# Routed experts computed on per-expert slot tiles instead of for every token

## The reference, cut to what matters

```
def _L2_ffn_ref(x, w_gate, wi_0, wi_1, wo):          # 8 experts, top 2, hidden 256
    logits = xf @ w_gate
    top_logits, top_idx = top_k(logits, 2)
    weights = softmax(top_logits)
    out = sum over the two experts e of a token:
          weights * ((silu(x @ wi_0[e]) * (x @ wi_1[e])) @ wo[e])

def _L3_ffn_ref(x, gate_w, shared_gate_w, shared_gate_up_w, shared_down_w, w13, w2):
    shared = (silu_and_mul(x @ shared_gate_up_w.T) @ shared_down_w.T) * sigmoid(x @ shared_gate_w.T)
    probs = softmax(x @ gate_w.T); routing_weights, selected = top_k(probs, 2)   # 8 experts, hidden 352
    out = shared + sum over e of w_e * (silu_and_mul(x @ w13[e].T) @ w2[e].T)
```

## Time and profile before

| | |
|---|---|
| median of 3 runs | 3531.37 us (3529.96 to 3534.61) |
| the profiled execution, its own time | 3534.85 us |
| its span (first to last instruction) | 3533.0 us |
| TensorE matmul busy | 3068.1 us, 87% |
| VectorE / ACT / GpSimd busy | 51% / 36% / 27% |
| mean granted TensorE clock | 0.932 |
| DMA | 185.23 MB, mean 52 GB/s |

### The profile page before, as it was taken

How to read it: one execution, slowest core, us unless ns; L and a number is a source line. 1 busy time by engine, 2 the same in 40 slices (tenths; PEclk the granted TensorE clock), 3 DMA queues, 4 the chain that set the end, 5 groups by cost and what they waited for, 6 DMA issues and landing times. The chain is left out here.

```text
span 3533.0 us, 39050 instructions
## 1 busy us (share of the span) xinstructions
PE 3068.1 (87%) x13170; PEld 1982.7 (56%) x13170; DVE 1811.0 (51%) x3116; ACT 1262.7 (36%) x2576; POOL 947.2 (27%) x331
## 2 busy tenths in 40 slices
PE   6997897998553999977999869997999879999998
PEld 3554685543232565545445347885555347777776
DVE  2443673776658998834565443334555432222222
ACT  0111221666246887701444422221444422221221
POOL 0000000885310101001666502210666602221220
PEclk9998998999876999988999879998999979999999
DMA  3220213423001001113212101103222102011100
GB/s 135 88 73 21 84 60 98 93 57 75 1 27 48 25 24 48 36 48 83 46 47 54 43 13 54 53 24 100 58 64 55 43 17 74 27 46 49 49 33 24
DMA packets 83282, 185.23 MB, mean 52 GB/s; under 512 B 19264, under 2 KB 23872, under 8 KB 81728
## 3 DMA queue, kind: packets, MB, share of 16 engines
q1 hardware_dynamic: 83136, 183.43, 17.6%
HBM read 122.30 MB, written 4.19 MB: 36 GB/s over the span
## 5 line engine op out<-in xcount | busy, mean ns | idle before, releaser
L429 PE MATMUL L_ffn_hidden<-L_ffn_x_high,L_ffn_up_high 128*128 128x512 f32 (+1 forms) x1344 | 553.7, 412 | 95.7 <-DVE L_ffn_routes L347 53.9
L1193 POOL TENSOR_TENSOR L_attn_total<-L_attn_total,L_attn_probs 128x2048 f32<-128x2048 f32 x120 | 547.4, 4561 | 150.4 <-ACT L_attn_probs L1148 146.1
L429 PE MATMUL L_ffn_hidden<-L_ffn_x_low,L_ffn_up_high 128*128 128x512 f32 (+1 forms) x1344 | 531.4, 395 | 0.0
L1227 DVE TENSOR_REDUCE L_attn_row_max<-L_attn_rows_ps 128x1 f32<-128x512 f32 x512 | 335.9, 684 | 269.3 <-PE L_attn_rows_ps L1034 266.3
L1148 ACT ACTIVATE L_attn_probs<-L_attn_s_ps 128x512 f32<-128x512 f32 x512 | 292.2, 596 | 421.9 <-PE L_attn_s_ps L1054 416.8
L429 PE MATMUL L_ffn_hidden<-L_ffn_x_high,L_ffn_up_low 128*128 128x512 f32 (+1 forms) x1088 | 432.3, 397 | 0.0
L1054 PE MATMUL L_attn_s_ps<-L_attn_q_stack,L_attn_k_stack 98*128 98x512 f32 (+1 forms) x768 | 379.3, 530 | 39.2 <-DMA L_attn_q_stack<-L_attn_ml 33.5
L295 POOL TENSOR_TENSOR L_ffn_up_low<-L_ffn_up_in,L_ffn_up_high 128x1408 fp32r<-128x1408 f32 (+2 forms) x48 | 153.5, 3199 | 912.9 <-ACT L_ffn_up_high L289 912.9
L549 DVE TENSOR_TENSOR L_ffn_product<-L_ffn_silu,L_ffn_hidden 128x512 f32<-128x512 f32 (+1 forms) x136 | 93.5, 687 | 588.9 <-ACT L_ffn_silu L484 588.9
L484 ACT ACTIVATE L_ffn_silu<-L_ffn_hidden 128x512 f32<-128x512 f32 x168 | 99.4, 592 | 700.7 <-PE L_ffn_hidden L429 644.1
L429 PEld LDWEIGHTS L_ffn_hidden<-L_ffn_x_high,L_ffn_up_high 128*128 128x128 f32 (+1 forms) x1344 | 250.9, 187 | 175.8 <-issue 73.4
(11 more groups left out here) (215 smaller groups left out, 4529.1 us busy)
## 6 DMA issues: line engine op xcount, KB each, us to landing
L_attn_k_stack<-L_attn_kh SPq DMA_DIRECT2D x192, 128.0 KB, 2.3
L_ffn_up_in<-in_L_ffn_w SPq DMA_DIRECT2D x24, 704.0 KB, 6.4
L_attn_ctxT<-in_ctxT SPq DMA_DIRECT2D x8, 2048.0 KB, 8.1
L_ffn_up_in<-in_L_ffn_w SPq DMA_DIRECT2D x32, 512.0 KB, 4.8
L_ffn_down_in<-in_L_ffn_w SPq DMA_DIRECT2D x28, 512.0 KB, 3.6
L_attn_abs_in<-in_L_ffn_w SPq DMA_DIRECT2D x12, 1024.0 KB, 8.8
L_attn_k_stack<-L_attn_kl SPq DMA_DIRECT2D x96, 128.0 KB, 2.4
L_attn_q_stack<-L_attn_qh SPq DMA_DIRECT2D x192, 64.0 KB, 2.0
```

The lines of the kernel that those rows point to most:

```text
L429: last = nc.tensor.matmul(hidden_ps[0:m, b, side, :], w[:, i, e0:e0 + m], x_parts[xp][:, i, h * HALF:(h + 1) * HALF], start=(q == 0), stop ...
L1193: nc.gpsimd.tensor_tensor(total[:], first, probs[:, g % P_SLOTS], ALU.add).then_inc(added, 1)
L1227: nc.vector.tensor_reduce(row_max[:, r // HALVES_K, r % HALVES_K:r % HALVES_K + 1], rows_ps[:, r % R_SLOTS, :], AX_X, ALU.max, negate=True ...
```

## The change

The two tokens-to-expert choices of each token become 2048 rows. Each expert gets whole tiles of 128 rows ("slots"), 23 slots in total at any routing ((2048 - 1) // 128 + 8).

- `norm_block` keeps all 8 normalised row tiles (`slots.rows`). In L2_ffn it no longer splits x, since no dense group is left.
- `expert_weights_block` counts, with 44 matmuls against a triangular and an all-ones matrix (after VectorE's `chosen`), each token's rank within its expert. VectorE turns these into a row number for each choice (`place`) and an expert for each slot (`expert_of`).
- GpSimd scatters the row tiles to `x_slots` in DRAM with 16 indirect DMAs (128 rows of 2 KB each): in L2_ffn at the end of the router's block, in L3_ffn as the `guest` at the head of its list in `ffn_block`.
- `routed_block` runs the 23 slots in plain fp32: load a tile of 128 rows, transpose it, gate and up products with the weights of the slot's expert, whose address TensorE reads into a register from `expert_of` (`value_load`), SiLU and product, transpose, down product, store to `y_slots`. All eight experts' weights lie in SBUF. Then GpSimd gathers the rows back with 16 indirect DMAs and VectorE adds each with its weight.
- L3_ffn runs `ffn_block` for the 4 shared groups only (G = 4), then `routed_block`. SP issues the routed weights at the start of that block, ahead of the x tiles; in L2_ffn it does so in the router's block.
- L0_attn's SP list gets 23 DMAs that write zeros to `x_slots` once.

```diff
+EXPERTS, PICKS = 8, 2
+SLOT_TILES = (TOK * PICKS - 1) // P + EXPERTS
...
+                    if guest:
+                        guest(pool)
                     group(0, 0)
...
+class Slots:
...
+        self.rows = sb("rows", [P, TILES, D])
+        self.place, self.weight = sb("place", [P, PICKS, TILES], U32), sb("pick_weight", [P, PICKS, TILES])
+        self.expert_of = sb("expert_of", [P, SLOT_TILES + 1], I32)
...
+    def scatter(self, env, pool):
+        pool.wait_ge(self.placed, 1)
+        for p in range(PICKS):
+            for t in range(TILES):
+                env.nc.gpsimd.indirect_dma_start(
+                    env.x_slots, bass.IndirectOffsetOnAxis(ap=self.place[:, p, t:t + 1], axis=0),
+                    self.rows[:, t, :], None).then_inc(self.scattered, 16)
...
+                pe.wait_ge(ones_made, 2)
+                pe.wait_ge(chosen, 1)
+                for t in range(TILES + 1):
+                    for u in range(min(t, TILES - 1) + 1):
+                        last = nc.tensor.matmul(rank_ps[:, t, :], before[:] if u == t else ones[:], both[:, u, :],
+                                                start=(u == 0), stop=(u == min(t, TILES - 1)))
+                last.then_inc(ranked, 1)
...
+                dve.wait_ge(ranked, 1)
+                link(nc.vector.tensor_tensor(over[:], rank_ps[:, TILES, :].unsqueeze(2).to_broadcast([P, EX, 8]),
+                                             bounds[:].unsqueeze(1).to_broadcast([P, EX, 8]), ALU.is_gt))
+                link(nc.vector.tensor_reduce(tiles_of[:], over[:], AX_X, ALU.add))
+                link(nc.vector.tensor_scalar(tiles_of[:], tiles_of[:], 1.0, None, ALU.max))
+                link(nc.vector.tensor_tensor(over[:], upto[:], tiles_of[:].unsqueeze(1).to_broadcast([P, EX, EX]), ALU.mult))
...
+                for p in range(PICKS):
+                    link(nc.vector.tensor_tensor(pick[:, p], pick[:, p], slot[:], ALU.mult), wait=(p == PICKS - 1))
+                link(nc.vector.tensor_reduce(at[:], pick[:], AX_X, ALU.add))
+                link(nc.vector.tensor_copy(slots.place[:], at[:]))
+                dve.sem_inc(slots.placed, 1)
...
+def routed_block(env, name, slots, weights, load_weights, E):
...
+                def load_x(i):
+                    if i >= XS:
+                        sp.wait_ge(x_turned, i - XS + 1)
+                    sp.dma_start(xg[:, i % XS, :], env.x_slots[i * P:(i + 1) * P, :]).then_inc(x_loaded[i % XS], 16)
+
+                def store_y(i):
+                    sp.wait_ge(y_copied, i + 1)
+                    sp.dma_start(env.y_slots[i * P:(i + 1) * P, :], y_sb[:, i % YS, :]).then_inc(stored[i % YS], 16)
+
+                load_weights(sp)
+                sp.wait_ge(slots.scattered, 16 * PICKS * TILES)
+                for i in range(XS):
+                    load_x(i)
+                for i in range(I):
+                    if i + XS < I:
+                        load_x(i + XS)
+                    store_y(i)
...
+                def turn_x(i):
+                    pe.wait_ge(x_loaded[i % XS], 16 * (i // XS + 1))
+                    if i >= 2:
+                        pe.wait_ge(x_copied, i - 1)
+                    for c in range(DC):
+                        last = nc.tensor.transpose(x_ps[:, i % 2, c, :], xg[:, i % XS, c * P:(c + 1) * P], env.ident[:])
+                    last.then_inc(x_turned, 1)
+
+                def up(i, expert, side):
+                    if side == 0:
+                        if i < EXPERTS:
+                            pe.wait_ge(slots.loaded[i], 16 * (2 + DOWN_LOADS))
+                        pe.wait_ge(x_copied, i + 1)
+                        if i >= 2:
+                            pe.wait_ge(hidden_done, i - 1)
+                    to, done = ((gate_ps, gate_done), (up_ps, up_done))[side]
+                    for c in range(DC):
+                        w = up_sb[:, bass.ds(expert, 1), side, c * E:(c + 1) * E].rearrange("p g e -> p (g e)")
+                        last = nc.tensor.matmul(to[:, i % 2, 0:E], xgT[:, i % 2, c, :], w, start=(c == 0), stop=(c == DC - 1))
+                    last.then_inc(done, 1)
+
+                def turn_hidden(i):
+                    pe.wait_ge(hidden_done, i + 1)
+                    if i:
+                        pe.wait_ge(h_copied, i)
+                    for c, m in enumerate(chunks):
+                        last = nc.tensor.transpose(h_ps[0:m, c, :], hidden[:, i % 2, c * P:c * P + m], env.ident[:])
+                    last.then_inc(h_turned, 1)
+
+                def down(i, expert):
+                    pe.wait_ge(h_copied, i + 1)
+                    if i:
+                        pe.wait_ge(y_copied, i)
+                    for c, m in enumerate(chunks):
+                        w = down_sb[0:m, bass.ds(expert, 1), c, :].rearrange("p g n -> p (g n)")
+                        last = nc.tensor.matmul(y_ps[:], hiddenT[0:m, i % 2, c, :], w, start=(c == 0), stop=(c == NCH - 1))
+                    last.then_inc(y_done, 1)
+
+                turn_x(0)
+                before = None
+                for i in range(I):
+                    expert = pe.value_load(slots.expert_of[0:1, i:i + 1], min_val=0, max_val=EXPERTS - 1)
+                    if i + 1 < I:
+                        turn_x(i + 1)
+                    up(i, expert, 0)
+                    if i:
+                        turn_hidden(i - 1)
+                    up(i, expert, 1)
+                    if i:
+                        down(i - 1, before)
+                    before = expert
+                turn_hidden(I - 1)
+                down(I - 1, before)
...
+                copy_x(0)
+                for i in range(I):
+                    if i + 1 < I:
+                        copy_x(i + 1)
+                    act.wait_ge(gate_done, i + 1)
+                    if i >= 2:
+                        act.wait_ge(hidden_done, i - 1)
+                    nc.scalar.activation(silu[:, i % 2, :], gate_ps[:, i % 2, 0:E], ACT.Silu).then_inc(silu_done, 1)
+                    if i:
+                        copy_hidden(i - 1)
+                copy_hidden(I - 1)
...
+                for n in range(YS):
+                    pool.wait_ge(stored[n], 16 * ((I - n + YS - 1) // YS))
+                for t in range(TILES):
+                    for p in range(PICKS):
+                        nc.gpsimd.indirect_dma_start(
+                            taken[p][:, t, :], None, env.y_slots,
+                            bass.IndirectOffsetOnAxis(ap=slots.place[:, p, t:t + 1], axis=0)).then_inc(back[PICKS * t + p], 16)
...
+                    nc.vector.tensor_copy(y_sb[:, i % YS, :], y_ps[:]).then_inc(y_copied, 1)
...
+                for t in range(TILES):
+                    for p in range(PICKS):
+                        n = PICKS * t + p
+                        dve.wait_ge(back[n], 16)
+                        if p:
+                            dve.wait_ge(added, n)
+                        nc.vector.scalar_tensor_tensor(env.x[:, t, :], taken[p][:, t, :], slots.weight[:, p, t:t + 1],
+                                                       env.x[:, t, :], ALU.mult, ALU.add).then_inc(added, 1)
+                dve.wait_ge(added, PICKS * TILES)
...
+                sp.wait_ge(blank_made, 1)
+                for i in range(SLOT_TILES):
+                    sp.dma_start(env.x_slots[i * P:(i + 1) * P, :], blank[:]).then_inc(blank_stored, 16)
...
+                def load_routed(sp, weights):
+                    up_sb, down_sb = weights
+                    for e in range(EXPERTS):
+                        g = shared + e
+                        for side, w in enumerate((w1, w2)):
+                            sp.dma_start(up_sb[:, e, side, :], w[g]).then_inc(slots.loaded[e], 16)
+                        sp.dma_start(down_sb[:, e, 0:full, :],
+                                     w3[g, 0:full * P, :].rearrange("(c p) n -> p c n", p=P)).then_inc(slots.loaded[e], 16)
+                        if E % P:
+                            sp.dma_start(down_sb[0:E % P, e, full, :], w3[g, full * P:E, :]).then_inc(slots.loaded[e], 16)
+
+                if shared:
+                    with ExitStack() as dense:
+                        weight = dense.enter_context(nc.sbuf_tensor(f"{name}_weight", [P, TILES, shared], F32))
+                        x_parts = x_halves(name, dense)
+
+                        def route(first):
+                            with nc.sbuf_tensor(f"{name}_xT", [P, DC, TOK], F32) as env.xT:
+                                norm_block(env, name, split=x_parts, rows=slots.rows)
+                                expert_weights_block(env, name, shared, normalise, gate, weight, first, slots)
+
+                        for n, w in (("w1", w1), ("w2", w2), ("w3", w3)):
+                            env.io[n] = w[0:shared]
+                        ffn_block(env, name, [min(P, E - c) for c in range(0, E, P)], weight, x_parts, meanwhile=route,
```

(11 more changed lines are left out.)

174 lines of the change are left out of this document (142 added, 32 removed).

## The result

| | before | changed |
|---|---|---|
| median of 4 runs each | 3532.05 us (3529.96 to 3534.61) | 3366.68 us (3363.94 to 3371.05) |
| the profiled execution, its own time | 3534.85 us | 3366.63 us |
| its span | 3533.0 us | 3364.9 us |
| TensorE matmul busy | 3068.1 us | 2767.1 us |
| mean granted TensorE clock | 0.932 | 0.907 |

The ratio is 0.9533, 95% interval [0.9516, 0.9549]: 165 us less. The forecast was 3385, its range 3320 to 3480; it was 18 us too high.

A forecast was written before the change was run, and what follows sets the result against it. TensorE alone was taken to bound the grouped matmuls of L2_ffn and L3_ffn. 3534.85 less 43.7 (L2_ffn) and 103.2 (L3_ffn) gave 3387.9, or 3385 us against the median of the runs; range 3320 to 3480.

The forecast's parts named there:

- ranks 19.0 us at clock 0.50: Rank matmuls after `chosen`: 44 matmuls, 88 instructions at the router's price of 0.216 us each, 19.0 us.
- I take 1.5: L2_ffn's 16 scattering DMAs on GpSimd: 1.5 us each, between 0.8 and 3.0, so 24 us plus 2.2 landing.
- I take 0.3 us, near the low end: Register load and register-addressed matmuls in each routed slot: 0.3 us a slot, between nothing and 1.8.
- 17.3 MB at 400 GB/s: L3_ffn's routed weights, loaded only after the dense part: 43.3 us, plus landing, barrier and first x tile, with TensorE idle.
- The interpolated price of a matmul with 352 columns: Up products in L3_ffn's slots: 0.30 us an instruction, on the line between 256 and 512 columns.
- 33.5 + 16.6: One dense group in L3_ffn: six up steps plus eight down tiles, written as 50.05 us; 8 of 12 groups go.
- sixteen scatters up to 1.9 us each: L3_ffn's GpSimd scatters ahead of group 1's low halves: hidden behind group 0 up to 1.9 us per DMA.
- The zeroing DMAs: 23 DMAs in L0_attn, 6 MB, 15 us at 400 GB/s, fall between SP's issues: cost nothing.
- (a): L3_ffn: x tiles don't queue behind the weights, TensorE starts some 7 us in; saves about 39 us, 3346; chance 0.08.
- (b): Routed slots: register load empties TensorE's queue, 1.8 instead of 0.3 us each; 69 us more, 3454; chance 0.18.
- (c): GpSimd's scatters and gathers are slower: gain gone at 3.9 us each, 3603 at 5 us; chance 0.09.
- (d): TensorE's clock stays at 0.50 in the routed slots: 322 us more, 3707; chance 0.04.

The follow-up runs named there:

- experiment 3: Changed kernel with TensorE loading each slot's expert number five times instead of once: 3388.96 us, ratio 0.9575 to the kernel before.
- experiment 4: Changed kernel with a constant expert per slot, no register load and no choice of weights by the routing: 3365.88 us, ratio 0.9515.
- experiment 10: The changed kernel run again unaltered, as yardstick on the same chip as the double scatter: 3365.37 us, ratio 0.9527.
- experiment 9: Changed kernel with each of the 32 scatters followed by a second one of the same rows to `y_slots`: 3400.46 us, ratio 0.9613.
- experiment 7: Changed kernel with L2_ffn computed as in the kernel before, L3_ffn as changed: 3423.51 us, ratio 0.9687.
- experiment 2: Changed kernel with L3_ffn's 32 routed weight loads issued by GpSimd, SP keeping x tiles and stores: 3334.11 us, ratio 0.9422.
- experiment 6: Changed kernel with scatters sending 64 rows instead of 128 and gathers fetching rows of 1 KB instead of 2 KB: 3359.94 us, ratio 0.95.
- experiment 5: Changed kernel with ranks counted by 9 matmuls instead of 44: 3337.72 us, ratio 0.9438.
- experiment 8: Changed kernel with the edits of experiment 2 and experiment 5 together: 3305.07 us, ratio 0.9345.
- experiment 11: Version of experiment 8 with GpSimd issuing an expert's weights only once the one two before has landed: 3303.38 us, ratio 0.9339.
- experiment 12: Version of experiment 8 run again unaltered, as yardstick on the same chip as experiment 11: 3301.65 us, ratio 0.934.

## Why the prediction was right, step by step

**L2_ffn: 263.4 forecast, 248.2 measured.** Norm +16.0 (+15.98), router +29.9 (+29.9), `chosen` +33.2 (+33.4), ranks 19.0 us at clock 0.50 (18.9): all from rows of the same shape, and all right. The step *"I take 1.5"* for a scattering DMA was too high: the pace is 1.27, and the first slot starts at +81.7, not +85.8. The step *"I take 0.3 us, near the low end"* for the register load was wrong: nothing of it shows (experiments 3 and 4). A slot is 5.83 us, where the matmul prices alone had given 5.88. That is 8.8 us over the slots. The tail is 28.2 instead of 30.5, again the price of a GpSimd DMA (1.37 us for a gather). Together 15.2 us too long.

**L3_ffn: 542.6 forecast, 536.9 measured.** Here errors cancelled in part. Slots: 8.08 instead of 8.43 us, 9.6 us too long in all; the tail 2.4 too long. Against that, the dense part ended at +268.8, not +266.1, and the gap behind it was 50.7 us, not 47.1. The first of these two is within what two executions differ by (+264.8 in experiment 10). The gap is 49.2 us there too: the step *"17.3 MB at 400 GB/s"* was mis-sized, the stretch has 347 GB/s. The interpolated price of a matmul with 352 columns, 0.30 us, was good: eight take 2.37 us in the chain. (The sum 33.5 + 16.6 is 50.1, not 50.05, which is 0.6 us over eight groups and changes nothing.) That sixteen scatters up to 1.9 us each are hidden there was right, and experiment 9 shows the bound from the other side.

**The rest.** The zeroing DMAs were put at nothing, and rightly: L1_ffn, the first sublayer that I timed behind them, begins at 964.71 where it began at 965.65. L2_ffn began 2.5 us later and L3_attn took 3.4 less, neither forecast. Experiment 10 has both again. Experiments 3 and 7 zero `x_slots` too and have the old 1121 us up to L2_ffn, so the zeroing isn't the cause; what is stays open.

**The rivals.** (a) *The x tiles don't queue behind the weights*: refuted as a forecast, with 51.49 us of idle TensorE. But its price was nearly real. Experiment 2 takes the tiles off that queue and gains 33 of the 39 us. (b) The register load doesn't empty the queue; with one load nothing shows, and more sequencer time than matmuls queued is there only with five. (c) GpSimd's DMAs at 1.27 and 1.37 us lie far below the break-even of 3.9. The figure for it that I gave from the Trainium skill, "GPSIMD Engine Reference", section "Performance pitfalls for Q7 kernels", 10.9 us for 128 indices, is not what this path pays: 64 indices more cost 0.054 us (experiment 6). (d) The clock rose to 1.00 within 5.3 us of the first slot of L2_ffn, and stayed. The 600 ns floor of a tensor_load from the Trainium skill, "DMA: Bandwidth & Descriptors", "Latency and other measured facts", isn't seen either, the trace has 0.300 us.

## What to carry to other kernels

A batch of fixed-price steps (ranks, scatter, gather) in front of and behind a shortened matmul phase gives back part of what the phase saved; price each by count times its fixed cost, and then ask for fewer of them, since here nine matmuls did the work of 44. Ask of every load on a path what stands ahead of it on its own queue: 256 KB behind 17.3 MB cost 42 us of idle TensorE, and moving the big loads to another queue gave most of it back. A register load on TensorE's sequencer was free here as long as the work already queued lasted longer than it.

## What the runs showed of the hardware

- An indirect DMA that scatters costs GpSimd 0.961 us for 128 rows of 2 KB and 0.907 for 64 rows, and 0.30 us pass between two (changed kernel, experiment 6). A plain one of 704 KB costs it 0.58 us (experiment 2).
- Behind its first twelve weight loads SP was held up to 3.19 us for one issue; GpSimd issued the same 32 DMAs in 19 us instead of 36 (changed kernel, experiment 2).
- A TENSOR_LOAD to a register on TensorE takes 0.300 us, with its arithmetic 0.47, and hides behind 1.72 us of queued matmuls (changed kernel, experiments 3 and 4).
- fp32 matmuls with 8, 9 and up to 72 columns take the same 0.22 us an instruction at clock 0.50 (changed kernel, experiment 5).
- A 256 KB load takes 2.8 us in the median, 8 to 10 while weights on another queue keep the engines busy, 13.9 behind the weights of its own (experiments 2, 8, 11, 12 and the changed kernel).
